# A fused attention and FFN block on one core: another order of the opening work (q and k projections of batch 0 ahead of the transposes of batch 1, GpSimd's rows of ones first)

## The chip, the core and the metric

The kernel runs on one core of a Trainium2 chip. The metric is the device time of one execution in microseconds. Five engines work in parallel, each with its own instruction stream in program order, and wait for each other through semaphores: TensorE (PE; matmuls and transposes), VectorE (DVE), ScalarE (ACT), GpSimd (POOL) and SyncE (SP), which here only issues DMA transfers.

## What is computed

Eight batches of 256 rows of width 256 go through a gated cross attention (16 heads of depth 16, keys and values from a context of the same shape) and then a gated FFN of inner width 704 whose activations and weights are rounded to 8 bit levels.

```python
# reference, cut to what matters
def attention(Q, K, V, Wq, Wk, Wv, Wo, bo):          # Q = layernorm(x), K = V = context
    q, k, v = Q @ Wq.T, K @ Wk.T, V @ Wv.T           # then split in 16 heads
    p = softmax(where(mask, q @ k.T / sqrt(16), -inf))
    return (p @ v) @ Wo.T + bo
x = x + tanh(g_xattn) * attention(layernorm(x), ctx, ctx, ...)
x = x + tanh(g_ffn) * ffn(layernorm(x))              # fake-quantised SiLU-gated FFN
return x
```

## The kernel before, in words

Everything is written by hand for each engine, with semaphores. Nothing reorders it: the order on each engine and in each DMA queue is the order in the code.

The stretch that the change touches is the prologue, from the first load to about 81 us: for each of the 8 batches b it normalises x, transposes normalised x and context, projects to q, k and v, and splits q and k in three bfloat16 parts. These are written to DRAM and read back in the layout of the heads. The parity p = b % 2 picks one of two buffers.

- VectorE: `stats(b)` (L781, L785: mean and variance, needs x of batch b loaded), `normalise(b)` (L791, needs GpSimd's 1/sqrt and writes `xn`, shown as arena), `ctx_copy(b)` (L797: transposed context from PSUM), and in `project(b)`: `normalise(b+2)`, `stats(b+3)`, the two residuals of q and k (L812), `ctx_copy(b+2)`. After every second batch `weight_amax` (L831) follows, which needs all FFN weights loaded.
- GpSimd: identity matrices, small constants, `project_rstd(b)` (six small instructions, L432 to L439), one memset of two rows of ones in the stacked keys (L460, shown as big), and the low parts of q and k (L449).
- TensorE: `weight_tr(n)` (L1123, the transpose of a weight matrix), `x_tr(b)` (L1131: transposes of xn, then L1137: those of the context, which wait for its load) and `project(b)`: q and k (L1173), v (L1184), then `x_tr(b+2)`. The q of batch b + 1 waits for the residual of q of batch b on VectorE (`res_done`), since both use the same PSUM bank.
- ScalarE: copies of the transposed weights (L580, L583) and of transposed xn (`xt_copy`, L588), then the high parts of q and k (L596), the middle parts (L601), the copy of v (L604). The high part of batch 2 waits for the write of batch 0's parts to DRAM, because it goes into the same buffer:

```python
                    if w == 0:
                        act.wait_ge(parts_out[p], 16 * j + 16)
```

- SyncE issues the loads in one fixed order. Some of them wait in the middle of the queue, and all that stands behind them waits too. The context of batch 3 goes into the buffer of that of batch 1, so it waits until TensorE has transposed batch 1's context. Behind it stand the small inputs, the FFN weights and x of batches 5 to 7. `x_load(7)` waits for x of batch 5 to have landed. Behind that stand Wo, the write of batch 0's parts (L378) and the context of batch 4:

```python
        def ctx_load(queue, b):
            if b >= 2:
                queue.wait_ge(ct_done, b - 1)
            queue.dma_start(ctx_rows[:, b % 2], ctx_dram[:, tiles(b)]).then_inc(c_in[b % 2], 16)
```

From `project(4)` on, TensorE and VectorE also make the first scores of batch 0 in between (`early_scores`, `maxima`), and from about 81 us the attention loop and then the FFN follow.

Of the kernel before, what the change touches and what calls it, by code (L numbers as in the profile page):

```python
# [66 lines left out]
def flamingo_block(nc, x, ctx_in, mask_rows, mask_full, g_xattn, g_ffn, Wq, Wk, Wv, Wo, bo,  # L67
# [17 lines left out]
    KR = 6 * D  # L85
    KM = KR + 2
# [29 lines left out]
    with ExitStack() as stack:  # L116
# [6 lines left out]
        def sem(name):  # L123
            return stack.enter_context(nc.semaphore(name))
# [56 lines left out]
        k_st = big[:, words:2 * words].bitcast(BF16).rearrange("p (a h s) -> p a h s", a=2, h=H)  # L181
# [51 lines left out]
        idents, consts, ones_rows = sem("idents"), sem("consts"), sem("ones_rows")  # L233
        w_tr, w_ready = sem("w_tr"), sem("w_ready")
# [51 lines left out]
        def tile(t):  # L286
            return slice(t, t + 1) if isinstance(t, int) else bass.ds(t, 1)
# [24 lines left out]
        def alone(engine):  # L312


            engine.sem_inc(carrier, 1)
# [100 lines left out]
        def _(pool):  # L416
# [4 lines left out]
            for m in (ident_f, ident_b):  # L421
                pool.affine_select(out=m[:], in_=m[:], compare_op=ALU.not_equal, fill=1.0, base=0,
                                   pattern=[[-1, P]], channel_multiplier=1).then_inc(idents, 1)
            chain.step(pool.memset(minus_half[:], -0.5))
            pool.sem_inc(rs2_ready, 1)
            pool.memset(wd_t[ILAST:P, IC - 1], 0.0).then_inc(pad_zero, 1)
# [29 lines left out]
            for b in range(3):  # L456
                project_rstd(b, b % 2)
            pool.wait_ge(rstd_done, 3)

            pool.memset(k_st[KR:KM].rearrange("r a h s -> r (a h s)").bitcast(mybir.dt.uint32), 0x3F803F80  # L460
                        ).then_inc(ones_rows, 1)
            pool.wait_ge(ones_rows, 1)
            with pool.Fori(0, 2) as i:
                chain.loop(i, 10)
                project(i * 2, 0)
# [300 lines left out]
        def _(dve):  # L766
# [9 lines left out]
            def stats(b, p, j):  # L776

                dve.wait_ge(x_in[p], j * 16 + 16)
                alone(dve)
                for c in range(QC):  # L780
                    chain.then(dve.bn_stats(stats1[:, p, c], x_rows[:, tile(b * QC + c)]))  # L781
                chain.wait()
                alone(dve)
                for c in range(QC):
                    done = dve.bn_aggr(mv1[:, p, c], stats1[:, p, c])  # L785
                done.then_inc(stats_done, 1)

            def normalise(b, p):
                dve.wait_ge(rstd_done, b + 1)
                for c in range(QC):  # L790
                    done = dve.tensor_scalar(xn[:, p, c], x_rows[:, tile(b * QC + c)].squeeze(1),  # L791
                                             mv1[:, p, c, 0:1], rs1[:, p, c:c + 1], ALU.subtract, ALU.mult)
                done.then_inc(xn_ready, 1)

            def ctx_copy(b, p):
                dve.wait_ge(ct_done, b + 1)
                dve.tensor_copy(ctx_t[:, p], bank_b[:, 2 + p]).then_inc(ctx_t_ready, 1)  # L797
# [40 lines left out]
            chain.then(dve.memset(h_max[:], 0.0))  # L838

            stats(0, 0, 0)  # L840
            normalise(0, 0)
            stats(1, 1, 0)
            normalise(1, 1)
            ctx_copy(0, 0)
            stats(2, 0, 1)
            ctx_copy(1, 1)
            with dve.Fori(0, 2) as i:
# [267 lines left out]
        def _(pe):  # L1115
# [51 lines left out]
            def project(b, p, j, ahead=True, heads=None):  # L1167
                for w, (src, ready, done) in enumerate(((xn_t, xn_t_ready, q_done), (ctx_t, ctx_t_ready, k_done))):
                    pe.wait_ge(ready, b + 1)
                    pe.wait_ge(res_done, 2 * b + w + 1)  # L1170
                    for f in range(EC):
                        for k in range(EC):
                            last = mm(bank_a[:, w, f * S:(f + 1) * S], w_t[:, w, k, f * P:(f + 1) * P],  # L1173
                                      src[:, p, k * S:(k + 1) * S], start=(k == 0), stop=(k == EC - 1))
                    last.then_inc(done, 1)
                    if heads:
                        early_scores(heads[w])
                pe.wait_ge(v_stored, b + 1)
                if heads and b == 6:
                    pe.wait_ge(gate_ready, 1)  # L1180
                    pe.wait_ge(full_ready, 1)
                for c in range(QC):
                    for k in range(EC):
                        last = mm(bank_o[:, c * E:(c + 1) * E], ctx_t[:, p, k * S + c * P:k * S + (c + 1) * P],  # L1184
                                  w_t[:, 2, k], start=(k == 0), stop=(k == EC - 1))
                last.then_inc(v_done, 1)
                if heads:
                    early_scores(heads[2])
                if ahead:
                    x_tr(b + 2, p, j + 1)  # L1190
                if heads:
                    early_scores(heads[3])
# [3 lines left out]
            x_tr(0, 0, 0)  # L1196
            pe.wait_ge(w_ready, 1)
            weight_tr(2)
            x_tr(1, 1, 0)
            pe.wait_ge(w_ready, 3)  # L1200
            with pe.Fori(0, 2) as i:
                project(i * 2, 0, i)
                project(i * 2 + 1, 1, i)
            weight_tr(3)
            project(4, 0, 2, heads=range(0, 4))
            project(5, 1, 2, heads=range(4, 8))
            pe.wait_ge(pad_ready, 1)
# [240 lines left out]
```

## Time and profile before

| | before |
|---|---|
| time, median of 3 runs | 318.63 us (318.26 to 318.68) |
| span of the profiled execution, first to last instruction | 315.9 us |
| TensorE matmuls busy in the span | 239.1 us (76%) |
| VectorE busy | 218.9 us (69%) |
| ScalarE busy | 176.1 us (56%) |
| GpSimd busy | 124.5 us (39%) |

The profile is of one execution. Its page gives the span, and no time of its own beside it; the median of the runs is 2.7 us longer than the span, which is what lies around the first and the last instruction. Busy shares are means over the prologue, the attention and the FFN, which have different limits. Only the first 81 us matter for what the change touches.

### The profile page before, as it was taken

The page shows a single profiled execution, that of the slowest core. Times are in us where ns is not written, and L with a number is a line of the kernel's source. Part 1 is how long each engine was busy: PE and PEld are TensorE (multiplying, and loading weights), DVE is VectorE, ACT ScalarE, POOL GpSimd, SP SyncE. Part 2 cuts the span into 40 slices and gives each one's busy share as a digit, 9 for nine tenths or more (in the row PEclk, how much of TensorE's full clock was granted, in tenths as well). Part 3 has the DMA queues.
Part 4 walks back from the last instruction along what each step waited for, and adds up shares of the span by engine and source line. Part 5 has one row for each costly group of instructions (what it writes and reads, how often), then busy time and mean ns, then how long its engine had stood idle before and what let it go on. Part 6 is the DMA issues. An engine that isn't in the chain of part 4 may idle for free.

```text
span 315.9 us, 6549 instructions
## 1 busy us (share of the span) xinstructions
PE 239.1 (76%) x1781; PEld 159.2 (50%) x1785; DVE 218.9 (69%) x465; ACT 176.1 (56%) x327; POOL 124.5 (39%) x213
## 2 busy tenths in 40 slices
PE   1799897999543999999999999999610578823951
PEld 1678676777322575757565656556400233312630
DVE  2579787765611769696979798894144389975992
ACT  2327583666711676676767667678501478836920
POOL 3366655232113135353434444353022395410074
PEclk9999999999955999999999999999875599995895
DMA  7767999933303353535353544000000000000025
GB/s 240 192 163 238 340 259 258 233 101 102 100 0 84 75 116 80 112 84 115 73 115 70 117 81 101 1 1 2 3 3 0 0 2 0 0 0 0 3 95 172
DMA packets 29734, 29.45 MB, mean 93 GB/s; under 512 B 5136, under 2 KB 26384, under 8 KB 29712
## 3 DMA queue, kind: packets, MB, share of 16 engines
q1 hardware_dynamic: 26832, 27.87, 34.8%
q10 hardware_dynamic: 2880, 1.31, 1.6%
q8 instruction: 11, 0.18, 0.2%
q14 instruction: 11, 0.09, 0.1%
HBM read 20.65 MB, written 8.39 MB: 92 GB/s over the span
## 4 chain that ended last, share of the span: by engine, by line
PE 27%; issue 14%; DVE 13%; POOL 6%; ACT 5%; DVEq 1%; DMA 1%; POOLq 0%; ACTq 0%; SPq 0%
PE bank_o L1281 6%; PE bank_a L1264 6%; PE bank_m L1307 5%; PE bank_b L1251 5%; DVE neg_max L801 3%; POOL x_rows L562 2%; PE bank_m L1289 2%; POOL arena L541 2%; PE bank_m L1297 2%; DVE x_rows L900 1%; ACT wgu_rows L761 1%; POOL big L553 1%; DVE arena L1076 1%; ACT big L662 1%; DVE stats L908 1%
## 5 line engine op out<-in xcount | busy, mean ns | idle before, releaser
L801 DVE TENSOR_REDUCE neg_max<-bank_b 128x2 f32<-128x512 f32 x112 | 73.9, 679 | 24.3 <-PE bank_b L1251 24.3
L662 ACT ACTIVATE big<-bank_a 128x512 f32<-128x512 f32 x128 | 69.8, 589 | 27.3 <-PE bank_a L1264 26.8
L1264 PE MATMUL bank_a<-big 98*128 98x256 bf16 x256 | 49.9, 278 | 9.5 <-DMA big<-max_parts 7.9
L1251 PE MATMUL bank_b<-big 96*128 96x256 bf16 x224 | 43.8, 277 | 0.0
L1281 PE MATMUL bank_o<-big,v_cur 128*32 128x256 f32 x512 | 35.8, 399 | 4.5 <-POOL v_cur L470 3.6
L1264 PEld LDWEIGHTS bank_a<-big 98*128 98x128 bf16 x256 | 21.4, 98 | 20.6 <-DMA big<-max_parts 8.4
L1173 PE MATMUL bank_a<-arena,w_t 128*128 128x256 f32 x128 | 31.1, 393 | 0.5 <-DVE resid L812 0.5
L476 POOL CAST max_parts<-max_f 8x256 bf16<-8x256 f32 x16 | 6.5, 405 | 56.0 <-ACT max_f L620 50.3
L1414 PE MATMUL bank_b<-wd_t,arena 128*128 128x256 bf16 x96 | 16.1, 323 | 14.4 <-DVE arena L1082 14.2
L1173 PEld LDWEIGHTS bank_a<-arena,w_t 128*128 128x128 f32 x128 | 24.4, 198 | 4.2 <-DVE resid L812 1.0
L449 POOL TENSOR_TENSOR arena<-resid,arena 128x512 bf16<-128x512 f32 x16 | 18.4, 1159 | 18.3 <-ACT arena L601 18.3
L1251 PEld LDWEIGHTS bank_b<-big 96*128 96x128 bf16 x224 | 21.9, 99 | 3.6 <-DVE neg_max L801 0.2
L1281 PEld LDWEIGHTS bank_o<-big,v_cur 128*32 128x32 f32 x512 | 13.8, 112 | 17.5 <-issue 6.4
L1414 PEld LDWEIGHTS bank_b<-wd_t,arena 128*128 x96 | 10.5, 110 | 20.0 <-issue 16.5
L738 ACT ACTIVATE arena<-bank_b,w_scale_x 128x512 f32<-128x512 f32 (+1 forms) x24 | 16.3, 685 | 7.6 <-PE bank_b L1397 5.2
L1397 PE MATMUL bank_b<-arena,wgu_t 128*128 (+3 forms) x61 | 17.8, 410 | 3.0 <-ACT arena L728 1.9
L761 ACT ACTIVATE wgu_rows<-big,magic,scal 128x768 f32 x16 | 14.8, 1013 | 7.7 <-DVE scal L1068 7.7
L1307 PE MATMUL bank_m<-w_t,arena 128*128 128x256 f32 x64 | 17.3, 418 | 1.1 <-ACT arena L673 1.1
L596 ACT ACTIVATE arena<-bank_a 128x512 bf16<-128x512 f32 x16 | 9.4, 595 | 15.7 <-PE bank_a L1173 9.2
L669 ACT ACTIVATE arena<-bank_o 128x256 f32<-128x256 f32 x32 | 12.3, 386 | 8.6 <-PE bank_o L1281 8.6
L900 DVE SCALAR_TENSOR_TENSOR x_rows<-bank_m,gate_x,x_rows 128x256 f32 (+1 forms) x16 | 7.0, 479 | 13.2 <-PE bank_m L1307 13.2
L562 POOL TENSOR_TENSOR x_rows<-x_rows,v_all x7 | 9.8, 1400 | 15.9 <-issue 15.7
(157 smaller groups left out, 473.0 us busy)
## 6 DMA issues: line engine op xcount, KB each, us to landing
qk_parts<-arena SPq DMA_DIRECT2D x8, 768.0 KB, 5.0
big<-qk_parts SPq DMA_DIRECT2D x32, 192.0 KB, 3.7
big<-qk_parts SPq DMA_DIRECT2D x32, 128.0 KB, 4.0
x_rows<-in_x SPq DMA_DIRECT2D x8, 256.0 KB, 5.4
big<-qk_parts SPq DMA_DIRECT2D x32, 64.0 KB, 4.0
out<-x_rows SPq DMA_DIRECT2D x8, 256.0 KB, 2.2
big<-in_ctx SPq DMA_DIRECT2D x7, 256.0 KB, 6.9
wd_rows<-in_L_ffn_w_down SPq DMA_DIRECT2D x1, 704.0 KB, 8.2
```

Source lines behind the costliest of these rows:

```text
L449: pool.tensor_tensor(parts[:, p, w, LO[w]], resid[:, p, w], parts[:, p, w, MID[w]], ALU.subtract).then_inc(lo_done, 1)
L662: act.activation(p_buf[:, h % HH], bank_a[:, h % 2].rearrange("p (c s) -> p c s", c=QC), ACT.Exp, scale=SCALE).then_inc(exp_done, 1)
L738: act.activation(silu[0:r, c % 3], bank_b[0:r, c % 3], ACT.Silu, scale=w_scale_x[0:r, c:c + 1]).then_inc(silu_done, 1)
L761: act.activation(h_round[:, q], h_all[:, :, bass.ds(t * P, P)], ACT.Identity, scale=INV_H, bias=magic[:]).then_inc(y_rounded, 1)
L801: dve.tensor_reduce(neg_max[:, p, :, h], bank.rearrange("p (c s) -> p c s", c=QC), axis=AX.X, op=ALU.max, negate=True).then_inc(max_done, 1)
L1173: last = mm(bank_a[:, w, f * S:(f + 1) * S], w_t[:, w, k, f * P:(f + 1) * P], src[:, p, k * S:(k + 1) * S], start=(k == 0), stop=(k == EC ...
L1251: done = mm(to, q_st[0:KR, p, h, c * P:(c + 1) * P], k_st[0:KR, p, h], start=True, stop=not masked)
L1264: done = mm(to, k_st[0:KM, p, h, k * P:(k + 1) * P], q_st[0:KM, p, h], start=True, stop=not masked)
L1281: done = mm(bank_o[n * 2 * D:(n + 1) * 2 * D, 0:S], v_cur[:, p, k, h], p_buf[:, h % HH, k], start=(k == 0), stop=(k == QC - 1))
L1307: done = mm(bank_m[:, c * E:(c + 1) * E], att_t[:, f, c * P:(c + 1) * P], w_t[:, 3, f], start=(f == 0), stop=(f == EC - 1))
L1397: last = mm(to, wgu_t[:, g, k, c * P:c * P + r], xq_t[:, k, bass.ds(n * CW, CW)], start=(k == 0), stop=(k == EC - 1))
L1414: last = mm(bank_b[:, 2 * p + q, c * E:(c + 1) * E], hq[:, f, bass.ds(b * S + c * P, P)], wd_t[:, f], start=(f == 0), stop=(f == IC - 1))
```

## The change

Four edits, all in the prologue.

1. GpSimd: the memset of the rows of ones stands right behind the identity matrices, and no longer between the `project_rstd` of batches 0 to 2 and the loop.
2. VectorE: `stats(1)` comes ahead of `normalise(0)`, and `ctx_copy(0)` ahead of `normalise(1)`.
3. TensorE: `x_tr(1)` moves from ahead of `project(0)` to between the k and the v of `project(0)`; the wait for three weight copies is split in two.
4. TensorE: the loop over the first four batches is written out.

```diff
@@ gpsimd
                 pool.affine_select(out=m[:], in_=m[:], compare_op=ALU.not_equal, fill=1.0, base=0,
                                    pattern=[[-1, P]], channel_multiplier=1).then_inc(idents, 1)
+            pool.wait_ge(idents, 4)
+            pool.memset(k_st[KR:KM].rearrange("r a h s -> r (a h s)").bitcast(mybir.dt.uint32), 0x3F803F80
+                        ).then_inc(ones_rows, 1)
+            pool.wait_ge(ones_rows, 1)
             chain.step(pool.memset(minus_half[:], -0.5))
...
             for b in range(3):
                 project_rstd(b, b % 2)
             pool.wait_ge(rstd_done, 3)
-
-            pool.memset(k_st[KR:KM].rearrange("r a h s -> r (a h s)").bitcast(mybir.dt.uint32), 0x3F803F80
-                        ).then_inc(ones_rows, 1)
-            pool.wait_ge(ones_rows, 1)
             with pool.Fori(0, 2) as i:
@@ vector
             stats(0, 0, 0)
+            stats(1, 1, 0)
             normalise(0, 0)
-            stats(1, 1, 0)
+            ctx_copy(0, 0)
             normalise(1, 1)
-            ctx_copy(0, 0)
             stats(2, 0, 1)
             ctx_copy(1, 1)
@@ tensor, project(b, p, j, ahead, heads), behind q and k
+                if isinstance(b, int) and b == 0:
+                    x_tr(1, 1, 0)
+                    pe.wait_ge(w_ready, 3)
                 pe.wait_ge(v_stored, b + 1)
@@ tensor
             weight_tr(2)
-            x_tr(1, 1, 0)
-            pe.wait_ge(w_ready, 3)
-            with pe.Fori(0, 2) as i:
-                project(i * 2, 0, i)
-                project(i * 2 + 1, 1, i)
+            pe.wait_ge(w_ready, 2)
+            for b in range(4):
+                project(b, b % 2, b // 2)
             weight_tr(3)
```

On TensorE, the opening of the program before: rows 3 and 4 are `x_tr(0)` (transposes of xn, then of the context), row 5 is `weight_tr(2)`, rows 6 and 7 `x_tr(1)`, and the L1173 rows q and k of batch 0.

```order
3 L1131 MATMUL bank_b<-ident_f,arena 128x128 x4
4 L1137 MATMUL bank_b<-ident_f,big 128x128 x4
5 L1123 MATMUL bank_o<-ident_f,arena 128x128 x4
6 L1131 MATMUL bank_b<-ident_f,arena 128x128 x4
7 L1137 MATMUL bank_b<-ident_f,big 128x128 x4
8 L1201 UNCONDITIONAL_BRANCH
9 L1201 ISA
10 L1170 ISA
11 L1173 MATMUL bank_a<-arena,w_t 128x256 x4
12 L1170 REGISTER_ALU
13 L1173 MATMUL bank_a<-arena,w_t 128x256 x4
```

The same place of the changed program:

```order
3 L1131 MATMUL bank_b<-ident_f,arena 128x128 x4
4 L1137 MATMUL bank_b<-ident_f,big 128x128 x4
5 L1123 MATMUL bank_o<-ident_f,arena 128x128 x4
6 L1173 MATMUL bank_a<-arena,w_t 128x256 x8
7 L1131 MATMUL bank_b<-ident_f,arena 128x128 x4
8 L1137 MATMUL bank_b<-ident_f,big 128x128 x4
9 L1187 MATMUL bank_o<-w_t,arena 128x256 x4
```

The eight projections of q and k now stand ahead of the transposes of batch 1, and the context transposes (L1137) that release SyncE's load of context 3 stand behind them.

On VectorE, the one piece of the difference (L781 and L785 are `stats`, L791 is `normalise`, L797 `ctx_copy`):

```order
 L781 BN_STATS stats<-x_rows 128x6 x2
 L785 BN_AGGR mv<-stats 128x2 x2
-L791 TENSOR_SCALAR arena<-x_rows,mv,rs 128x256 x2
 L781 BN_STATS stats<-x_rows 128x6 x2
 L785 BN_AGGR mv<-stats 128x2 x2
 L791 TENSOR_SCALAR arena<-x_rows,mv,rs 128x256 x2
 L797 COPY arena<-bank_b 128x512
+L791 TENSOR_SCALAR arena<-x_rows,mv,rs 128x256 x2
```

`normalise(0)` now stands behind `stats(1)`, which needs x of batch 1, and `normalise(1)` behind the copy of context 0. ScalarE's and SyncE's instructions are the same in both programs.

## Rows read from the trace of the kernel before

**Rows 1.** Timeline, VectorE, 8 to 25 us (start, duration, instruction, idle time before)

```profile
8.21 0.74 DVE L791 TENSOR_SCALAR arena<-x_rows,mv,rs 128x256 f32<-128x256 f32 x2 [2.66 <-POOL rs L439]
8.86 0.75 DVE L781 BATCH_NORM_STATS2 stats<-x_rows 128x6 f32<-128x256 f32 x2
9.76 0.25 DVE L785 BATCH_NORM_AGGREGATE mv<-stats 128x2 f32<-128x6 f32 x2
...
17.65 3.55 DVE L791 TENSOR_SCALAR arena<-x_rows,mv,rs 128x256 f32 x1 [1.59 <-POOL rs L439]
...
22.49 1.26 DVE L812 TENSOR_TENSOR resid<-bank_a,arena 128x512 f32<-128x512 f32 x2
```

**Rows 2.** Timeline, GpSimd, 2 to 22 us

```profile
2.07 0.31 POOL L426 MEMSET wd_t<- 64x256 bf16 x1 [0.15 <-POOL minus_half L424]
5.77 0.26 POOL L432 TENSOR_SCALAR newton<-mv 128x2 f32<-128x2 f32 x1 [3.39 <-DVE mv L785]
...
7.98 0.20 POOL L439 TENSOR_TENSOR rs<-rs,newton 128x2 f32<-128x2 f32 x1 [0.18 <-POOL newton L437]
...
17.54 3.51 POOL L460 MEMSET big<- 2x4096 uint32 x1
```

**Rows 3.** Timeline, TensorE matmuls, 9 to 27 us

```profile
9.01 1.12 PE L1131 MATMUL bank_b<-ident_f,arena 128*128 128x128 f32 x4 [0.71 <-DVE arena L791]
...
10.77 1.06 PE L1123 MATMUL bank_o<-ident_f,arena 128*128 128x128 f32 x4
13.36 1.11 PE L1131 MATMUL bank_b<-ident_f,arena 128*128 128x128 f32 x4 [1.54 <-DVE arena L791]
...
15.13 4.96 PE L1173 MATMUL bank_a<-arena,w_t 128*128 128x256 f32 x16
...
23.21 3.72 PE L1173 MATMUL bank_a<-arena,w_t 128*128 128x256 f32 x16 [0.52 <-DVE resid L812]
```

**Rows 4.** Timeline, SyncE's queue of DMA issues, 15 to 34 us

```profile
15.36 0.38 SPq L304 DMA_DIRECT2D big<-in_ctx  x1
...
21.58 8.58 SPq L329 DMA_DIRECT2D x_rows<-in_x  x3
...
30.79 0.40 SPq L378 DMA_DIRECT2D qk_parts<-arena  x1
31.23 1.94 SPq L304 DMA_DIRECT2D big<-in_ctx  x1
```

**Rows 5.** DMA issues at 1.87 us: size, time from issue to landing

```profile
x_rows<-in_x SPq DMA_DIRECT2D x1, 256.0 KB, 6.7
```

**Rows 6.** DMA issues at 21.58 us and at 30.79 us, the same columns

```profile
x_rows<-in_x SPq DMA_DIRECT2D x1, 256.0 KB, 8.2
...
qk_parts<-arena SPq DMA_DIRECT2D x1, 768.0 KB, 5.1
```

**Rows 7.** Timeline, all engines, 35 to 45 us

```profile
35.91 1.08 ACT L596 ACTIVATE arena<-bank_a 128x512 bf16<-128x512 f32 x2 [3.54 <-DMA qk_parts<-arena]
...
36.67 0.66 PE L1137 MATMUL bank_b<-ident_f,big 128*128 128x128 f32 x4 [1.52 <-DMA big<-in_ctx]
...
43.64 0.69 DVE L797 COPY arena<-bank_b 128x512 f32<-128x512 f32 x1 [0.67 <-PE bank_b L1137]
```

**Rows 8.** Timeline, GpSimd, at 87 us

```profile
87.14 0.40 POOL L515 PARTITION_ALL_REDUCE scal<-scal  x1 [6.07 <-issue]
```

**Rows 9.** Stretches of 1 us: engines' busy times, TensorE's granted clock, DMA share, GB/s

```profile
86.00:87.00 1.00, 0.00 (x0) 0.00 (x0) 0.00 (x0) 0.00 (x0) 0.00 (x0) 0.55 0.00 0
...
103.00:104.00 1.00, 1.00 (x14) 0.56 (x7) 0.00 (x0) 0.21 (x1) 0.00 (x0) 0.91 0.57 90
```

**Rows 10.** Timeline, TensorE matmuls, 84 to 101 us

```profile
84.15 0.38 PE L1251 MATMUL bank_b<-big 96*128 96x256 bf16 x2
88.15 1.93 PE L1281 MATMUL bank_o<-big,v_cur 128*32 128x256 f32 x16 [3.62 <-POOL v_cur L470]
...
99.83 0.60 PE L1264 MATMUL bank_a<-big 98*128 98x256 bf16 x2 [7.93 <-DMA big<-max_parts]
```

## The prediction

> **What bounds the kernel now.** I read the timelines of the five engines for the first 45 us one beside the other, then the queue of SyncE's DMA issues, because a change of order in a prologue is worth only what the last wait lets through. The question at each place is: who was waited for last?
>
> At the start it is latency. VectorE normalises batch 0 at 8.21 us after 2.66 us of waiting for GpSimd; TensorE transposes at 9.01, is idle for 1.54 us and transposes batch 1 at 13.36, and q and k of batch 0 begin only at 15.13 [rows 1, 3]. At 17.54 GpSimd's memset runs for 3.51 us, and one `normalise` on VectorE, started 0.11 us later, takes 3.55 us [rows 1, 2]: it is held up by the memset, and the residual of batch 0 comes only at 22.49. TensorE's q of batch 1 waits for it until 23.21 [rows 1, 3]. These are the places that the change attends to.
>
> But the prologue is not paced there. At 35.91 ScalarE has waited 3.54 us for the write of batch 0's parts to land, and at 36.67 TensorE has waited 1.52 us for the context of batch 4 [rows 7]. Both transfers stand in SyncE's queue behind the loads of x: they are issued at 30.79 and 31.23 [rows 4]. They are that late for two reasons, of which one follows the other. The load of x of batch 7 waits for x of batch 5, issued at 21.58 and landed 8.2 us later, at 29.78, behind the FFN weights; the row of three loads that begins at 21.58 is 8.58 us long for this [rows 4, 6]. And the queue came to x of batch 5 at 21.58 because the load of context 3, at 15.36, had waited for TensorE's transposes of context 1; from there to 21.58 the issues follow each other without a wait [rows 4]. The transposes ended at about 15.33: 13.36, then 8 of them at the rate of the x16 row (15.13 is where the next work begins, and the last one ends some 0.2 us behind) [rows 3].
>
> So the number to follow is the end of batch 1's context transposes. Each microsecond that it moves moves 15.36, 21.58, 29.78, 30.79, and 35.91 and 36.67 with it.
>
> **The change, part by part.**
>
> *VectorE's order.* x of batch 1 is issued at 1.87 and lands 6.7 us later, at 8.57 [rows 5]. `stats(1)` ran at 8.86 and hence never showed this wait. Now it stands ahead of `normalise(0)`. It takes 8.86 to 10.01, that is 1.15 us [rows 1], so it runs from about 8.6 to 9.8, and `normalise(0)` starts at 9.8 instead of 8.21: **1.6 us later**. In front of it VectorE stands idle, and behind it queue TensorE's first transposes: 10.6 instead of 9.01.
>
> *GpSimd's memset.* It starts at about 1.95 and ends at 5.45; the two small memsets behind it (the second 0.31 us long) end at about 6.05 [rows 2], against a start of `project_rstd(0)` at 5.77. The chain of six takes 5.77 to 8.18, 2.41 us [rows 2], so it ends at 8.5, and `normalise(0)` isn't there before 9.8. The cover is 1.3 us. Should the memset also hold up VectorE's small memsets and `stats(0)` until 5.45, which no row shows, `stats(0)` would start 1 us late, the chain would end at 9.2, and that is still inside the cover. Cost 0 from both sides. `project_rstd(1)` runs from 9.8 to 12.2, and its `normalise(1)` comes at 13.3 behind `ctx_copy(0)`, well before TensorE wants it.
>
> *TensorE's order.* From 9.01 to the end of `weight_tr(2)` were 2.8 us (10.77 + 1.06), its issue done 0.2 us earlier [rows 3]. Now q starts at 10.6 + 2.6 = 13.2. The 16 matmul records of q and k took 4.96 us at 15.13, but 3.72 us at 23.21 [rows 3]: in the first the engine went from its lower level (1.2 GHz) to the upper one (2.4 GHz) on the way. (The granted clock column has no value below 1.00 this early; the durations tell the level: four transposes take 1.06 us here.) The upper level alone is about 3.4 us of issue, the lower alone twice that, 6.8. In the old order the excess of 1.24 us over 3.72 us says that some 2.5 us of this row were at the lower level, so the clock rose at about 17.7, 4.4 us after TensorE had begun to work without a gap at 13.36. Now there is no gap from 10.6 on; the same 4.4 us give a rise at 15.0, and q and k end at 13.2 + 3.4 + (15.0 - 13.2) / 2 = 17.5. The transposes of batch 1 take 0.9 us at the upper level (half of the 1.8 us between 13.36 and 15.13) and end at 18.4. Against 15.33 that is **3.1 us later**. Bounds: a rise at 14.0 gives 17.9, that is +2.6; a rise at 18.0 gives 19.8, that is +4.5.
>
> *What becomes of the gain in front.* With the memset gone from 17.54, VectorE does `ctx_copy(1)` at 18.5, `normalise(2)` at 19.1, `stats(3)`, and the residual of batch 0 at about 21.1 instead of 22.49. ScalarE has to copy xn of batch 1 (`xt_copy(1)`) ahead of the high part of q, and does so at about 18.0, so that isn't late. TensorE's q of batch 1 starts 1.3 us earlier. That lead is gone at batch 2: ScalarE then waits for the write of batch 0's parts, issued at 30.79 + 3.1 = 33.9 and landed 5.1 us later [rows 6], at 39.0 instead of 35.9.
>
> *What the longer wait does to the clock.* TensorE stood still for 1.52 us before 36.67. Now it is done with v of batch 2 about 1.3 us earlier, while the context of batch 4 comes 3.1 us later, at 39.8. In between stand only the transposes of xn of batch 4, behind `weight_amax` on VectorE, which waits for the FFN weights (3.1 us later too). So there are two stretches without work, the second 4 us or more. Further down in the trace TensorE is idle from 84.5 to 88.15, and the granted clock falls at 86.1 (0.55 in the stretch 86 to 87 is 0.1 us at 1.00 and 0.9 us at 0.50) [rows 9, 10]. Work resumes at 99.83 and the clock rises at about 103.2, 3.3 us later [rows 9, 10]. I therefore expect a fall before 39.8, and a return 3.3 to 4.4 us after it, as in the two places above. Half of that, 1.65 to 2.2 us, is lost on TensorE. VectorE waits for TensorE at the copy of context 5 (43.64, 0.67 us of waiting [rows 7]), and from there it is busy or waited for, so the loss goes through, less the 0.2 us or so by which q of batch 3 has to wait for the residual anyway: **+1.7 us**. Bounds: 0 if the clock stays up, 3 if it stays low for 6 us.
>
> The Trainium skill, page "TensorE: Matmul & The Clock Gate", part 1, says that the lower level is what an idle TensorE falls back to and that activity releases it. The trace agrees at 86.1 and 103.2. By that rule this change, which lengthens an idle stretch, pays for the clock too; without it the sum would end at +3.1.
>
> *From there to the end.* The rest of the prologue is a chain over TensorE, ScalarE and VectorE, with no transfer at a fixed time. It ends with GpSimd's last low part at 81.1, and then GpSimd needs 6.07 us before its all-reduce at 87.14, for which the profile names no other engine [rows 8], and TensorE waits until 88.15 [rows 10]. All of it is relative to the chain, so a delay at 44 us is a delay at the end. The loop written out on TensorE changes only six control rows; I count it at 0.
>
> **Sum.** 3.1 + 1.7 = 4.8 us, on a span of 315.9: 320.7. With the 2.7 us between span and median that is 323.4 us.
>
> **The rivals.**
>
> - *The clock does not fall, or its fall is hidden.* In favour: in the first stretch of waiting (1.52 us) it did not fall, and VectorE's chain of 44 to 51 us might be the later one. Against: the idle stretch is now over twice as long as the one after which it fell. +3.1: 321.7 us.
> - *The clock stays low longer at both ends.* Rise at 18 us in the opening (+4.5) and 6 us low after 39.8 (+3): 326.1 us.
> - *Faster.* The lead of 1.3 us at batch 1 passes on, if SyncE's queue isn't what makes batch 2 wait. It decides at batch 2: the write of batch 0's parts would have to be issued before about 29.5. For this the context transposes of batch 1 must end before 14, which q and k in front of them rule out by these rows; only if x of batch 5 landed early for its later issue (the DMA engines idle more before) could it be near. 318.6 - 1.3 = 317.3 us.
> - *The shift is absorbed.* Loads that are issued later find a free queue, and x of batch 5 lands 3 us sooner after its issue. Against: FFN weights and x of batch 5 were all issued within 3 us after a quiet stretch then too, so the 8.2 us are the transfer's own. 318.6 us.
>
> **How the numbers follow.** Both terms 0.54 (own range 322.3 to 325); shift without clock 0.24; longer low clock 0.12; faster 0.06; absorbed 0.04. The measurement tells 0.2% (0.6 us) from no change. Slower by more holds the first three, 0.90; faster 0.06; same 0.04. The range from 320.9 (shift of 2.6 and little for the clock) to 325.9 leaves out both last cases and the end of the third.
>
> **What would show it.** Right: `normalise(0)` behind `stats(1)` at 9.8; the context transposes of batch 1 end near 18.4; SyncE's context 3 then; the write of batch 0's parts at 33.9; ScalarE's high part of batch 2 at 39.0 after a wait of some 8 us; granted clock 0.50 around 39 to 44; all-reduce near 92. Wrong: the FFN weights' loads starting before 18 us, a write of batch 0's parts before 31, or an attention loop that starts less than 2 us later.

## The result, and the profile after

| | before | changed |
|---|---|---|
| time, median | 318.65 us (318.26 to 318.90, 4 runs) | 321.87 us (320.62 to 322.39, 4 runs) |
| ratio to before | | 1.0102, 95% interval 1.0059 to 1.0146 |
| span of the profiled execution | 315.9 us | 320.1 us |
| mean granted TensorE clock | 0.906 | 0.892 |

The changed kernel is 3.2 us slower. The timeline of the changed kernel, in the order of time (start, duration, engine, instruction, idle time before and what ended it); these lines answer to [rows 1, 3, 4, 7, 8, 10]:

```profile
8.33 0.75 DVE L781 BATCH_NORM_STATS2 stats<-x_rows 128x6 f32<-128x256 f32 x2 [2.50 <-DMA x_rows<-in_x]
...
9.39 0.70 DVE L791 TENSOR_SCALAR arena<-x_rows,mv,rs 128x256 f32<-128x256 f32 x2
...
12.76 5.08 PE L1173 MATMUL bank_a<-arena,w_t 128*128 128x256 f32 x16
...
18.12 0.60 PE L1137 MATMUL bank_b<-ident_f,big 128*128 128x128 f32 x4
...
18.75 0.38 SPq L304 DMA_DIRECT2D big<-in_ctx  x1
...
21.06 1.26 DVE L812 TENSOR_TENSOR resid<-bank_a,arena 128x512 f32<-128x512 f32 x2
...
25.10 8.33 SPq L329 DMA_DIRECT2D x_rows<-in_x  x3
...
34.05 0.40 SPq L378 DMA_DIRECT2D qk_parts<-arena  x1
34.50 1.56 SPq L304 DMA_DIRECT2D big<-in_ctx  x1
...
39.48 1.09 ACT L596 ACTIVATE arena<-bank_a 128x512 bf16<-128x512 f32 x2 [8.54 <-DMA qk_parts<-arena]
...
40.20 1.12 PE L1137 MATMUL bank_b<-ident_f,big 128*128 128x128 f32 x4 [4.46 <-DMA big<-in_ctx]
41.11 4.57 PE L1173 MATMUL bank_a<-arena,w_t 128*128 128x256 f32 x16
...
48.31 0.69 DVE L797 COPY arena<-bank_b 128x512 f32<-128x512 f32 x1 [1.28 <-PE bank_b L1137]
...
91.33 0.40 POOL L515 PARTITION_ALL_REDUCE scal<-scal  x1 [5.59 <-issue]
...
103.35 0.61 PE L1265 MATMUL bank_a<-big 98*128 98x256 bf16 x2 [7.25 <-DMA big<-max_parts]
```

Read the starts against those of before. Up to the residual of batch 0 the front is ahead: 21.06 instead of 22.49. SyncE's queue is behind: context 3 at 18.75 instead of 15.36, the first of the three loads of x at 25.10 instead of 21.58, the write of batch 0's parts at 34.05 instead of 30.79. The two waits that ended last before are longer, 8.54 us instead of 3.54 on ScalarE and 4.46 us instead of 1.52 on TensorE. Then the row of q and k of batch 3 takes 4.57 us, which before took 3.72. The copy of context 5 is 4.67 us late (43.64 to 48.31), the all-reduce 4.19 and the attention loop's restart 3.52 (99.83 to 103.35).

Stretches of 1 us of the changed kernel: busy times of PE, PEld, DVE, ACT and POOL, then the granted clock, DMA share and GB/s.

```profile
35.00:36.00 1.00, 0.66 (x4) 0.42 (x4) 0.85 (x5) 0.00 (x0) 0.00 (x0) 1.00 0.89 270
36.00:37.00 1.00, 0.00 (x0) 0.00 (x0) 0.08 (x2) 0.00 (x0) 0.64 (x2) 0.60 1.12 346
40.00:41.00 1.00, 0.80 (x4) 0.81 (x5) 0.90 (x2) 0.73 (x3) 0.00 (x0) 0.50 1.14 347
43.00:44.00 1.00, 1.00 (x6) 0.87 (x5) 1.00 (x3) 1.00 (x2) 0.81 (x1) 0.99 1.02 194
```

TensorE's last work before the wait ends at 35.7. In the stretch 36 to 37 the mean clock is 0.60 (1.00 for 0.2 us, then 0.50), in 40 to 41 it is 0.50 (the lower level, 1.2 GHz), in 43 to 44 it is 0.99. Work had resumed at 40.20. Before, TensorE waited at the same place too, but shorter, and the clock stayed at 1.00.

### The profile page after: what moved, and what is told of

It is laid out like the page before. It is cut to its first block, busy times and chain, and to the rows that moved or that the text cites. A ratio compares the mean times of both kernels' runs of the same rounds, so it can differ in the third digit from the quotient of the medians.

```text
span 320.1 us, 6539 instructions
## 1 busy us (share of the span) xinstructions
PE 240.3 (75%) x1785; PEld 159.6 (50%) x1785; DVE 215.8 (67%) x465; ACT 176.0 (55%) x327; POOL 124.8 (39%) x213
## 4 chain that ended last, share of the span: by engine, by line
PE 27%; issue 14%; DVE 13%; POOL 7%; ACT 4%; DVEq 1%; DMA 1%; POOLq 0%; ACTq 0%; SPq 0%
PE bank_o L1282 6%; PE bank_a L1265 6%; PE bank_m L1308 5%; PE bank_b L1252 5%; DVE neg_max L801 3%; POOL x_rows L562 2%; POOL arena L541 2%; PE bank_m L1290 2%; POOL big L553 2%; PE bank_m L1298 2%; DVE x_rows L900 1%; ACT wgu_rows L761 1%; DVE arena L1076 1%; ACT big L662 1%; PE bank_m L1145 1%
## 5 line engine op out<-in xcount | busy, mean ns | idle before, releaser
L801 DVE TENSOR_REDUCE neg_max<-bank_b 128x2 f32<-128x512 f32 x112 | 73.9, 679 | 23.7 <-PE bank_b L1252 23.7
L1173 PE MATMUL bank_a<-arena,w_t 128*128 128x256 f32 x128 | 32.1, 402 | 0.6 <-DVE resid L812 0.6
L1173 PEld LDWEIGHTS bank_a<-arena,w_t 128*128 128x128 f32 x128 | 25.3, 206 | 4.2 <-issue 0.8
L453 POOL TENSOR_TENSOR arena<-resid,arena 128x512 bf16<-128x512 f32 x16 | 18.4, 1161 | 20.7 <-ACT arena L601 20.7
L1282 PEld LDWEIGHTS bank_o<-big,v_cur 128*32 128x32 f32 x512 | 13.8, 112 | 17.1 <-issue 6.6
L1398 PE MATMUL bank_b<-arena,wgu_t 128*128 (+3 forms) x64 | 18.7, 412 | 2.5 <-ACT arena L728 1.6
L812 DVE TENSOR_TENSOR resid<-bank_a,arena 128x512 f32<-128x512 f32 x16 | 10.7, 685 | 9.6 <-ACT arena L596 9.6
```

The costliest lines, as they stand in the source:

```text
L453: pool.tensor_tensor(parts[:, p, w, LO[w]], resid[:, p, w], parts[:, p, w, MID[w]], ALU.subtract).then_inc(lo_done, 1)
L801: dve.tensor_reduce(neg_max[:, p, :, h], bank.rearrange("p (c s) -> p c s", c=QC), axis=AX.X, op=ALU.max, negate=True).then_inc(max_done, 1)
L1282: done = mm(bank_o[n * 2 * D:(n + 1) * 2 * D, 0:S], v_cur[:, p, k, h], p_buf[:, h % HH, k], start=(k == 0), stop=(k == QC - 1))
L1398: last = mm(to, wgu_t[:, g, k, c * P:c * P + r], xq_t[:, k, bass.ds(n * CW, CW)], start=(k == 0), stop=(k == EC - 1))
```

## The experiments

Each kernel was timed beside the kernel before on the same chip. In these timings the executions of one kernel lay further apart than in the first (before: 315.5 to 321.9 us), so the ratios have intervals of about 0.3 to 0.5% to each side, and I read the traces beside them. The ratio on record is not simply the quotient of the two medians; the two differ by up to 0.4%. I go by the ratio and its interval. In some kernels of this section lines of code are added or left out, so a line number can be one or two (in the filler kernel up to eight) off those of before.

**1. Each engine's edit alone.**

GpSimd's edit on the kernel before:

```diff
+            pool.wait_ge(idents, 4)
+            pool.memset(k_st[KR:KM]...
             chain.step(pool.memset(minus_half[:], -0.5))
...
             pool.wait_ge(rstd_done, 3)
-            pool.memset(k_st[KR:KM]...
```

> The kernel before with one edit of the change: GpSimd's memset of ones as its opening work. Theory (SyncE's queue decides): normalise(2) on VectorE no longer takes 3.5 us, the residual of batch 0 comes 1 to 2 us earlier, but the write of batch 0's parts is still issued at 30.8 us and the time stays at 318.6 (0.6 either way). Rival (the prologue's latency decides): the lead of about 1 us arrives at the end, 317.5 or less. A second rival: VectorE's small memsets and the first statistics are held up until 5.5 us by the memset.

Measured: 319.63 us against 318.30, ratio 1.0048 (1.0010 to 1.0085). Timeline of this kernel:

```profile
14.99 0.38 SPq L304 DMA_DIRECT2D big<-in_ctx  x1
...
18.14 0.73 DVE L792 TENSOR_SCALAR arena<-x_rows,mv,rs 128x256 f32 x2 [2.10 <-POOL rs L443]
19.85 1.26 DVE L813 TENSOR_TENSOR resid<-bank_a,arena 128x512 f32<-128x512 f32 x2
...
30.28 0.40 SPq L378 DMA_DIRECT2D qk_parts<-arena  x1
...
35.91 1.08 ACT L597 ACTIVATE arena<-bank_a 128x512 bf16<-128x512 f32 x2 [6.19 <-DMA qk_parts<-arena]
...
36.62 1.11 PE L1138 MATMUL bank_b<-ident_f,big 128*128 128x128 f32 x4 [3.93 <-DMA big<-in_ctx]
37.53 4.74 PE L1174 MATMUL bank_a<-arena,w_t 128*128 128x256 f32 x16
```

`normalise(2)` takes 0.73 us where it took over 3.5, and the residual comes 2.6 us earlier. All of this is gone at 35.91, the very start of before: ScalarE waits 6.19 us instead of 3.54. And TensorE, which is done earlier too, now idles 3.93 us instead of 1.52; its q and k of batch 3 take 4.74 us instead of 3.72. A gain in front of a fixed wait became a longer idle stretch and a slower clock behind it, and VectorE's copy of context 5 comes at 44.91, 1.3 us later than before. I had expected no change of the time; the interval lies just above 1. That the clock makes this small loss is not shown: the profiled execution, at 317.70 us the fastest of its kernel, has the same span as that of before, 315.9 us. The Trainium skill, page "SBUF — State Buffer", section "Who interferes with whom", says that a `tensor_scalar` on VectorE can need a port pair that GpSimd holds for a whole instruction, and then fully waits. The trace agrees: 3.55 us with the memset beside it [rows 1, 2], 0.73 us for both halves without. The rival that VectorE's small memsets would be held up in the opening is refuted by the changed kernel: its statistics of batch 0 begin at 4.68 us, in the middle of GpSimd's memset, and what ended the wait before them is the load of x.

VectorE's order alone:

```diff
             stats(0, 0, 0)
+            stats(1, 1, 0)
             normalise(0, 0)
-            stats(1, 1, 0)
+            ctx_copy(0, 0)
             normalise(1, 1)
-            ctx_copy(0, 0)
```

> The kernel before with VectorE's new order alone. Theory: normalise(0) starts at about 9.4 instead of 8.2, because stats(1) waits for x of batch 1, and TensorE's first transposes move by 1.1 us; but the transposes of batch 1 wait for normalise(1) in both orders, at about 13.5, so the context load of batch 3 is issued within 0.3 us of the old 15.4 and the time stays within 0.5 us of before. Rival (the wait for x of batch 1 is what makes the change slow): 1 us slower.

Measured: 317.63 us against 318.30, ratio 0.9976 (0.9942 to 1.0011): no difference that can be told. Its timeline:

```profile
9.54 0.70 DVE L791 TENSOR_SCALAR arena<-x_rows,mv,rs 128x256 f32<-128x256 f32 x2
...
12.91 0.72 DVE L791 TENSOR_SCALAR arena<-x_rows,mv,rs 128x256 f32<-128x256 f32 x2
...
14.82 0.37 SPq L304 DMA_DIRECT2D big<-in_ctx  x1
```

`normalise(0)` is 1.3 us later than in [rows 1], as forecast, and it doesn't matter in this order, since `normalise(1)` is what the transposes of batch 1 wait for. It comes 0.3 us later, and context 3 is even issued 0.5 us earlier, at 14.82, since in this execution the transposes ran at the upper level already (four in 0.60 us).

TensorE's order alone (with `x_tr(1, 1, 0)` and the wait for `w_ready` 3 ahead of v in `project`, as in the change):

```diff
             weight_tr(2)
-            x_tr(1, 1, 0)
-            pe.wait_ge(w_ready, 3)
-            with pe.Fori(0, 2) as i:
-                project(i * 2, 0, i)
-                project(i * 2 + 1, 1, i)
+            pe.wait_ge(w_ready, 2)
+            for b in range(4):
+                project(b, b % 2, b // 2)
```

> The kernel before with TensorE's new order alone (transposes of batch 1 between k and v of batch 0, loop written out). Theory: the context load of batch 3 is issued at 17.5 to 18.5 us instead of 15.4, the write of batch 0's parts 2 to 3 us later, TensorE's idle stretch before the context of batch 4 grows to 3.5 us or so; 2.3 us slower if the clock stays up, 3.5 us if it falls: 321 to 322. Rival (VectorE's order is the costly part): under 1 us slower.

Measured: 322.34 us against 318.30, ratio 1.0105 (1.0066 to 1.0144). This edit alone, with the loop written out, loses as much as the whole change (1.0102). Its timeline:

```profile
17.77 0.38 SPq L304 DMA_DIRECT2D big<-in_ctx  x1
...
33.59 0.40 SPq L378 DMA_DIRECT2D qk_parts<-arena  x1
...
39.36 1.12 PE L1137 MATMUL bank_b<-ident_f,big 128*128 128x128 f32 x4 [3.23 <-DMA big<-in_ctx]
40.27 6.15 PE L1173 MATMUL bank_a<-arena,w_t 128*128 128x256 f32 x16
...
49.06 0.69 DVE L797 COPY arena<-bank_b 128x512 f32<-128x512 f32 x1 [1.28 <-PE bank_b L1137]
```

Context 3 is 2.4 us late, the write 2.8 us, and q and k of batch 3 take 6.15 us.

**2. All edits but VectorE's order,** on the changed kernel:

```diff
             stats(0, 0, 0)
-            stats(1, 1, 0)
             normalise(0, 0)
-            ctx_copy(0, 0)
+            stats(1, 1, 0)
             normalise(1, 1)
+            ctx_copy(0, 0)
```

> The changed kernel with VectorE's old order (normalise(0) ahead of stats(1), normalise(1) ahead of ctx_copy(0)). Theory, as in the prediction: TensorE starts 1.1 to 1.6 us earlier, the context load of batch 3 is issued at 17.6 to 18 us, and the kernel is about 1 us faster than the changed one and still 2 to 3 us slower than before. Rival (VectorE's order doesn't matter): the time of the changed kernel.

Measured: 321.41 us against 317.17, ratio 1.0137 (1.0095 to 1.0180). The time doesn't show the 1 us. Timeline:

```profile
17.36 0.37 SPq L304 DMA_DIRECT2D big<-in_ctx  x1
...
33.36 0.40 SPq L378 DMA_DIRECT2D qk_parts<-arena  x1
```

The queue is 1.4 us earlier at context 3 and 0.7 us at the write than in the profile of the changed kernel. This alone doesn't show that VectorE's wait for x of batch 1 pushes the queue. Six profiles of this study have the whole opening of the change (the changed kernel twice, with filler, and with three other queues). In them TensorE's transposes of batch 0 begin at 9.76 to 10.39 us, here at 9.52, so VectorE's old order can be worth 0.2 to 0.9 us there. But the transposes of context 1 end anywhere from 17.1 to 19.1 us in the six, because the row of q and k takes from 3.87 to 5.25 us, depending on when the clock rises in that execution. Context 3 at 17.36 is within this spread. What VectorE's order is worth in the queue and at the end stays open.

**3. The clock.** The changed kernel with work of no use where TensorE waits:

```diff
+            def filler(n):
+                for _ in range(n):
+                    tr(bank_m[:, 0:P], ident_f[:], ident_f[:])
             def x_tr(b, p, j):
+                if isinstance(b, int) and b == 4:
+                    filler(16)
                 pe.wait_ge(xn_ready, b + 1)
...
+                if isinstance(b, int) and b == 4:
+                    filler(38)
                 pe.wait_ge(c_in[p], 16 * j + 16)
```

> The changed kernel with 54 transposes of the identity matrix into an unused bank, placed where TensorE waits for xn and context of batch 4 (16 ahead of the one wait, 38 ahead of the other); they compute nothing that is used. Theory: the granted clock stays at 1.00 from 18 us on, q and k of batch 3 take 3.7 us again, and 1.0 to 1.3 us of the change's loss come back: about 320.6. Rival (the clock costs nothing, another engine is later): the time of the changed kernel, 321.9, or longer by what the filler delays.

Measured: 320.80 us against 318.30, ratio 1.0060 (1.0027 to 1.0093). Timeline, then one stretch of 4 us:

```profile
17.15 0.38 SPq L304 DMA_DIRECT2D big<-in_ctx  x1
...
34.09 0.40 SPq L378 DMA_DIRECT2D qk_parts<-arena  x1
...
34.19 4.31 PE L1129 MATMUL bank_m<-ident_f 128*128 128x128 f32 x38
40.46 0.66 PE L1145 MATMUL bank_b<-ident_f,big 128*128 128x128 f32 x4 [1.95 <-DMA big<-in_ctx]
...
47.55 0.69 DVE L797 COPY arena<-bank_b 128x512 f32<-128x512 f32 x1 [0.73 <-PE bank_b L1145]
```

```profile
38.00:42.00 4.00, 1.95 (x13) 1.42 (x12) 1.62 (x3) 1.98 (x4) 0.19 (x1) 1.00 1.08 315
```

The clock stayed at 1.00. The stretch that the clock stretches can be read from the traces alone, as the time from TensorE's start on context 4 to VectorE's copy of context 5: before 43.64 - 36.67 = 6.97 us, with filler 47.55 - 40.46 = 7.09, changed 48.31 - 40.20 = 8.11, TensorE's order alone 49.06 - 39.36 = 9.70. On this stretch the fall of the clock thus costs 1.1 to 2.7 us, and the filler takes all of it away. The two ratios (1.0060 and 1.0102) stand as that would have it, 1.3 us apart, but their intervals overlap, so the times alone don't show it.

The filler touches nothing ahead of batch 4, and yet context 3 was issued at 17.15 here and at 18.75 in the changed kernel, while the write went out at the same time (34.09 and 34.05). x of batch 5 took 9.6 us to land in this execution and 7.9 in that one. So a microsecond at context 3 doesn't always arrive at the write: in the other seven profiles with the old queue the write follows context 3 by 15.1 to 16.0 us, here by 16.9.

**4. The changed kernel again,** timed beside the next three kernels:

> The changed kernel once more, beside the variants of this call on the same chip: 1.0% slower than before, as in its first timing.

Measured: 323.46 us against 318.62, ratio 1.0113 (1.0063 to 1.0164). Here the ratio and the medians lie furthest apart: 1.13% is 3.6 us, and the medians differ by 4.8 us. The loss is there again, and its size is known to about 1.6 us either way.

**5. SyncE's queue.** First, context 3 behind the gate and up weights (on the changed kernel):

```diff
             x_load(4)
-            ctx_load(sp, 3)
...
+            ctx_load(sp, 3)
             sp.dma_start(wd_rows[:], w_down...
```

> The changed kernel with one line of SyncE's queue moved: the load of context 3 stands behind the loads of the gate and up weights instead of ahead of the small inputs. Theory (the change's loss is that the queue waits for the transposes of context 1): the loads behind it no longer wait, x of batch 5 is issued at about 20 us and lands at 28, the write of batch 0's parts is issued at about 29 us instead of 34, and the kernel is at least 2 us faster than before, 4 us or more faster than the change. Rival (TensorE's own new order or VectorE's wait for x of batch 1 is the loss): within 1 us of the changed kernel.

Measured: 318.07 us against 318.62, ratio 0.9976 (0.9940 to 1.0012). One moved line takes back all of the loss, with all edits on the engines in place, so the loss is the queue's. But it isn't 2 us faster than before, as I had expected. Timeline:

```profile
19.62 9.68 SPq L329 DMA_DIRECT2D x_rows<-in_x  x3
29.35 0.66 SPq L299 DMA_DIRECT2D arena<-in_L_xattn_Wo  x1
30.12 0.40 SPq L378 DMA_DIRECT2D qk_parts<-arena  x1
...
35.98 0.66 PE L1137 MATMUL bank_b<-ident_f,big 128*128 128x128 f32 x4 [3.41 <-DMA big<-in_ctx]
36.71 5.38 PE L1173 MATMUL bank_a<-arena,w_t 128*128 128x256 f32 x16
```

x of batch 5 is issued 5.5 us earlier than in the changed kernel, but the row of three loads lasts 9.68 us instead of 8.33, and the write is only 3.9 us earlier, at 30.12. One more load (context 3) now stands close ahead of x of batch 5, but whether that makes the row longer isn't shown: with filler and the old queue it lasted 10.00 us. And TensorE, faster in front, still idles 3.41 us and gets a slow row of 5.38 us.

Next, x of batches 5 and 6 ahead of the weights as well, on both kernels:

```diff
             x_load(4)
-            ctx_load(sp, 3)
+            x_load(5)
             for n, v in enumerate((g_xattn, g_ffn, clip_x, clip_down)):
...
+            x_load(6)
             for g, w in enumerate((w_gate, w_up)):
...
+            ctx_load(sp, 3)
             sp.dma_start(wd_rows[:], w_down...
...
-            for b in range(5, B):
-                x_load(b)
+            x_load(7)
```

> The changed kernel with x of batches 5 and 6 also ahead of the FFN weights in SyncE's queue. Theory: the write of batch 0's parts is issued as soon as GpSimd has made the low parts, at 26 to 27 us, ScalarE's high part of batch 2 starts at about 32 instead of 39.5, TensorE's clock doesn't fall there; 4 us faster than before, 314.5. Rival (the transfers themselves are the limit, since the FFN weights still have to come in between): the write is issued early but lands after 34; 2 us faster than before.

> The same order of SyncE's queue on the kernel before. Theory: the write is issued at 27.4 us (low parts ready then), high part of batch 2 at about 33; 3 us faster than before, and 1 to 1.5 us slower than the changed kernel with this queue, because now the lead of the front arrives at the end. Rival (the front never matters): both kernels with this queue take the same time.

Measured: changed kernel with this queue 315.14 us, ratio 0.9875 (0.9836 to 0.9914); kernel before with this queue 316.14 us, ratio 0.9915 (0.9879 to 0.9951). Both are faster than before; between them the intervals overlap, so whether the lead of the front arrives at the end is left open by this pair. On the kernel before the write is issued at 27.54 and ScalarE's high part starts at 32.50 without a wait, as expected. In the changed kernel with this queue the write is issued at 24.93, and yet (its timeline, and the DMA issues at 24.9: size, time to landing):

```profile
24.93 0.39 SPq L379 DMA_DIRECT2D qk_parts<-arena  x1
...
33.37 1.08 ACT L597 ACTIVATE arena<-bank_a 128x512 bf16<-128x512 f32 x2 [3.53 <-DMA qk_parts<-arena]
```

```profile
qk_parts<-arena SPq DMA_DIRECT2D x1, 768.0 KB, 8.4
```

It lands after 8.4 us instead of 5.1 [rows 6]. The down weights (issued at 19.71) landed 9.0 us later, at 28.7, and Wo (21.30) at 30.0, so both were still on their way when the write was issued. So the rival had a part of it: the transfers were the next limit.

Last, the weights right behind x of batch 4, ahead of the stretch in which the DMA engines stood idle (0 GB/s from 16 to 19 us in the changed kernel; before that, from 13 to 15 us, they moved up to 351 GB/s, so "idle from 12 us on" below is too much), then x of 5 and 6, context 3, the small inputs, x of 7. The queue's code from x of batch 4 on:

```python
            x_load(4)
            for g, w in enumerate((w_gate, w_up)):
...
            sp.dma_start(wd_rows[:], w_down...
            x_load(5)
            x_load(6)
            ctx_load(sp, 3)
            for n, v in enumerate((g_xattn, g_ffn, clip_x, clip_down)):
...
            x_load(7)
            w_load(sp, 3, Wo)
```

> The changed kernel with a second order of SyncE's queue: behind x of batch 4 come the FFN weights at once (the DMA engines idle from 12 us on), then x of 5 and 6, context 3, the small inputs, x of 7. Theory: the weights have landed by 21 us, the write of batch 0's parts is issued at about 25 and lands 5 us later in a free queue instead of 8.4, high part of batch 2 at 31 instead of 33.4; 5 us or more faster than before (313.5), and faster than the same queue on the kernel before by the lead of the front, 1.3 us. Rival (front lead absorbed by another wait): both the same.

> The same second order of the queue on the kernel before. Its engines had no DMA wait between 20 and 45 us with the first queue any more, so it should be no faster than with that: 316, 0.8% faster than before.

Measured: changed kernel with this queue 312.83 us against 317.17, ratio 0.9849 (0.9812 to 0.9887); kernel before with it 316.15 us, ratio 0.9957 (0.9929 to 0.9985). The changed kernel's timeline and the landing of its write:

```profile
26.42 0.39 SPq L379 DMA_DIRECT2D qk_parts<-arena  x1
...
31.73 1.08 ACT L597 ACTIVATE arena<-bank_a 128x512 bf16<-128x512 f32 x2 [0.39 <-DMA qk_parts<-arena]
```

```profile
qk_parts<-arena SPq DMA_DIRECT2D x1, 768.0 KB, 5.3
```

The wait of 8.54 us at this place is down to 0.39 us. This is the fastest kernel of the study, 1.5% faster than before. And with this queue the change itself is a gain: 0.9849 against 0.9957, intervals apart, about 1.1% (3.3 us between the medians). That is more than the 1.3 us of lead that I had put on it. Between the two profiles the lead is 1.4 us at the copy of context 5 (40.98 and 42.35). It is 1.9 us at the next residual, ahead of which ScalarE waits 1.94 us for a write of parts in the kernel before and 0.38 in the changed one. At the all-reduce it is 2.2 us (83.97 and 86.17), and 3.0 us on the span. So 2.2 of the 3.0 us arise ahead of the all-reduce; where the rest comes from stays open.

**6. The queue late, and nothing else.** On the kernel before:

```diff
             sp.dma_start(tg_bo[:], bo.partition_broadcast(P)).then_inc(small_in, 16)
+            for n in range(7):
+                sp.dma_start(late_t[:, n:n + 1], g_xattn.partition_broadcast(P)).then_inc(late, 16)
```

> The kernel before, all engines in their old order, with seven extra loads of 128 numbers (into a tile that nothing reads) in SyncE's queue behind the small inputs: 7 issues of 0.47 us put everything behind them 3.3 us later, and nothing else is touched. Theory (the change's loss is SyncE's queue plus the clock): the write of batch 0's parts is issued at 34 us, ScalarE's high part of batch 2 starts at 39, TensorE's idle stretch grows to over 4 us and its clock falls; 3 to 4.5 us slower than before, the same as the change. Rival (the new order on the engines costs something of its own): under 2 us slower.

Measured: 326.48 us against 317.17, ratio 1.0296 (1.0255 to 1.0338). Timeline, and a stretch of 4 us:

```profile
18.72 3.28 SPq L347 DMA_DIRECT2D late_t<-in_g_xattn  x7
...
29.98 9.73 SPq L330 DMA_DIRECT2D x_rows<-in_x  x3
...
40.35 0.40 SPq L381 DMA_DIRECT2D qk_parts<-arena  x1
...
45.90 1.08 ACT L599 ACTIVATE arena<-bank_a 128x512 bf16<-128x512 f32 x2 [13.01 <-DMA qk_parts<-arena]
...
54.66 0.69 DVE L800 COPY arena<-bank_b 128x512 f32<-128x512 f32 x1 [1.28 <-PE bank_b L1140]
```

```profile
24.00:28.00 4.00, 4.00 (x20) 3.51 (x20) 4.00 (x6) 3.87 (x7) 3.35 (x7) 1.00 0.05 0
```

The seven issues took the 3.28 us that I had counted, but the write was 9.56 us late and not 3.3: the issues behind them stood still as well (below). The size of my expectation was wrong by a factor of three, since it priced the issues and not the transfers. For the question the kernel is a clear answer: 9.6 us at the write gave 9.3 us between the medians, with no engine's order touched. The rival, that the new order on the engines costs something of its own, isn't needed. The clock fell here too (8.10 us from TensorE's start on context 4 at 46.56 to the copy of context 5, against 6.97), and the copy is 11.0 us late. On the span 8.7 us of it are left, so the clock's part doesn't show at the end of this kernel.

## Why the prediction was right, step by step

- *The number to follow is the end of batch 1's context transposes.* Right. Predicted 18.4, measured 18.7; the load of context 3 was issued at 18.75, 3.4 us late where 3.1 was forecast. TensorE's edit alone and the one moved line show the queue's wait for these transposes as the cause, and the late queue that a late write is enough for such a loss. That the end agrees to 0.3 us is luck in part: with the same opening it lay between 17.1 and 19.1 us in six profiles. And it doesn't move everything behind it one for one, as the kernel with filler shows.
- *VectorE's order: 1.6 us later.* 1.2 us (9.39 instead of 8.21). x of batch 1 landed 6.3 us after its issue, not 6.7. Alone it was worth nothing. With TensorE's new order its share, in the queue and at the end, is smaller than what the moment of the clock's rise changes from one execution to the next, and stays open (experiment 2).
- *GpSimd's memset: 0 from both sides.* Its start at 1.93 and the chain behind it, which ended at 8.72 (8.5 forecast), were hidden behind `stats(1)`. The gain that it brings in front is in the sum only as a longer wait of TensorE, in the clock term. What I hadn't expected is that alone it measured 0.5% slower.
- *TensorE's order.* q from 12.76 (13.2 forecast), then 4.92 us until the next work (4.3 forecast, since I let the clock rise earlier, at 15.0 where the durations say about 15.5); the two errors nearly cancel. The step behind it, that the clock rises 4.4 us after TensorE began to work without a gap, doesn't hold: here it is about 5.4 us, with filler about 3 (q and k take 3.87 us from 12.37 on), and with GpSimd's edit alone the transposes at 13.87 ran at the upper level right behind a gap of 1.53 us. The bounds (+2.6 and +4.5) were the better part of this term.
- *The lead is gone at batch 2.* Right: residual at 21.06 (21.1 forecast), write at 34.05 (33.9), ScalarE's high part at 39.48 (39.0).
- *The clock: +1.7.* It fell at 36.2 and rose at 43.0 (clock rows above), 2.8 us after work resumed, where 3.3 to 4.4 was forecast; with TensorE's order alone it was 6.0. On the stretch up to the copy of context 5 it costs 1.1 us in this profile, 2.6 in the second one of the changed kernel and 2.7 with TensorE's order alone. The term lies between them, and which one comes varies from execution to execution. What of it is left at the end of the kernel no timing shows clear of the noise.
- *From there the delay goes through.* 4.67 us at the copy of context 5 against 4.8 forecast; 4.2 us on the span. In between GpSimd's two gaps without a named releaser were shorter than before: 5.59 us ahead of the all-reduce instead of 6.07, and 7.09 us behind it instead of 7.76, so that the restart at 103.35 comes only 3.5 us late. Over the kernels of this study the first gap is 5.5 to 6.2 us and the second 6.7 to 7.8; the profile of before has the longest second one. I found no edit that explains them, and their cause stays open.
- *The loop written out: 0.* Never run alone. The kernels with context 3 or the weights moved contain it and aren't slower than before, which leaves little room for a cost.
- *The sum.* 320.7 for the span, measured 320.1. On the time I was 1.5 us too high, 323.4 against 321.87. I had taken 2.7 us for what lies around the first and the last instruction, and that is wrong: wherever an execution has both numbers, its time is 1.7 to 1.9 us longer than its span (321.85 - 320.1 = 1.75 us for the profiled one of the changed kernel). By this the profiled execution of the kernel before took about 317.7 us and was 1 us faster than the median, and the 4.2 us between the two spans are 1 us more than the 3.2 us between the medians. So the close agreement on the span is luck in part. The forecast of +4.8 us was too high: the first timing gives 3.2 us (1.9 to 4.7), the second by its ratio 3.6 (2.0 to 5.2). The way, the cause and the order of size were right; which term is too large, 3.1 or 1.7, the times can't tell.
- *The rivals.* Faster through the lead: refuted as the change stands, and true once the queue is in another order. Absorbed because the loads find a free queue: x of batch 5 landed 7.9 us after its issue instead of 8.2, so no. The clock does not fall: it fell, though the measured 321.87 us lie nearer to this rival's 321.7 than to the forecast. Low for longer at both ends: not in the profile of the changed kernel (+3.4 and 1.1 us); the second half of it came close in others, with 2.6 and 2.7 us.

## What to carry to other kernels

Before an order on a compute engine is changed, ask which transfers are released by the work that is put back, and what stands behind them in the same queue. Here one load waited for a buffer's release, though TensorE uses its data only at 27.57 us, and with it waited fifteen other issues ahead of the write that mattered. A prologue whose first batch was made faster became longer at the end. And time won ahead of a wait that doesn't move isn't neutral: it lengthens TensorE's idle stretch, and the clock may fall in it. And a time read from one profile, as the end of these transposes, can be 2 us off in the next execution of the same code; the shift that two profiles show is only as good as that.

## What the runs showed of the hardware that I had not expected

- Seven loads that spread one number over 128 partitions (0.5 KB each) took 7.3 us from issue to landing as a median, and the DMA engines moved next to nothing from 24 to 28 us (0 GB/s in the row above), though gate and up weights had been issued at 22.5 and 23.6; their landing took 10.6 and 11.7 us, and SyncE's own issue of the up weights at 23.60 lasted 3.54 us, where before it was 0.58. The four such loads of the kernel itself took 2.5 to 3.0 us in the same run. Why the seven are so slow together I didn't test.
- A row of three loads that was begun 5.5 us earlier ended only 4.1 us earlier, and a 768 KB write issued at 24.9 took 8.4 us to land where one issued at 26.4, when the FFN weights had landed (the last at 23.7), took 5.3. In these runs moving an issue forward moved the landing by less when other transfers were still under way.
- TensorE's clock fell after 1.6 us without work in [rows 9, 10], within 0.5 us of the last matmul in the changed kernel (which had also waited 1.73 us just ahead of it), and not at all in the 1.5 us of before's wait. With TensorE's order alone it fell 2.4 us after the last matmul. With context 3 behind the weights it stayed up through 3.41 us of waiting and fell at about 37.4, 1.4 us after work had resumed (mean clock 0.71 in the stretch 37 to 38). So the idle time just ahead of it doesn't tell by itself whether or when it falls.
